# A decoder of twelve stages on one core: an opening with plain-f32 value tiles, codebook weights decoded a stage earlier, and a narrow cross-attention that works in pairs of tiles

## What is computed

```python
def _L2_xattn_ref(q, k, v, w_q, w_k, w_v, w_out, mask):      # 32 heads of 16, 8 key/value groups
    query, key, value = q @ w_q.T, k @ w_k.T, v @ w_v.T
    ...
    scores = jnp.einsum('bghnd,bgsd->bghns', query, key) / D_HEAD ** 0.5
    scores = jnp.where(mask, scores, jnp.finfo(scores.dtype).min)
    attention = jax.nn.softmax(scores, axis=-1)
    out = jnp.einsum('bghns,bgsd->bghnd', attention, value)
    return out.transpose(0, 3, 1, 2, 4).reshape(b, n, D_MODEL) @ w_out.T

def _L3_xattn_ref(hidden_states, cross_attention_states, attention_mask, ...):   # 32 heads of 128, 8 groups
    q, k, v = ...                                            # projections, then rmsnorm of q and k
    scores = jnp.einsum('bhqd,bhkd->bhqk', q, k) * scale + attention_mask
    attn = jax.nn.softmax(scores.astype(jnp.float32), axis=-1)
    out = jnp.einsum('bhqk,bhkd->bhqd', attn, v)
    return out... @ o_proj_w.T

def _L3_ffn_ref(x, codebooks, bias, ln_weight, codes, centroids):
    cw = _expand(centroids, codebooks)                       # 32 centroids, looked up in codebooks
    dots = x2 @ cw.T                                         # then normalised, softmax, > 0.5
    qmask, cmask = jnp.any(m, axis=-1), jnp.any(m, axis=0)
    W = _expand(codes, codebooks)                            # 512 x 512 weights, looked up too
    y = x2 @ W.T + bias
    return y * (qmask[:, None] & kmask[None, :])
```

## Time and profile before

| what | value |
|---|---|
| three runs | 1671.37, 1674.64, 1674.88 us; median 1674.64 |
| the profiled execution | 1671.8 us, its span 1670.0, mean granted clock 0.984 |
| PE busy | 1556.8 us (93%), 7321 matmuls |
| DVE busy | 1012.7 us (61%) |
| ACT busy | 889.4 us (53%) |
| POOL busy | 364.9 us (22%) |
| DMA | 165.38 MB, mean 99 GB/s |

### The profile page before, as it was taken

How to read it: one execution, slowest core, us unless ns; L and a number is a source line. 1 busy time by engine, 2 the same in 40 slices (tenths; PEclk the granted TensorE clock), 3 DMA queues, 4 the chain that set the end, 5 groups by cost and what they waited for, 6 DMA issues and landing times. The chain is left out here.

```text
span 1670.0 us, 22556 instructions
## 1 busy us (share of the span) xinstructions
PE 1556.8 (93%) x7321; PEld 1153.7 (69%) x7321; DVE 1012.7 (61%) x2105; ACT 889.4 (53%) x1625; POOL 364.9 (22%) x312
## 2 busy tenths in 40 slices
PE   7999999999998989898889996997999999999986
PEld 5878777877874444586566664875777787777864
DVE  3036777776676863374388873655067667766663
ACT  4235666555655441364158884552266667666661
POOL 0001111110112330153146663540011011111010
PEclk9999999999999999998999998999999999999999
DMA  9431222111165008262362202536311112211012
GB/s 311 128 114 57 83 75 82 57 57 57 50 252 194 26 26 296 87 213 72 93 153 30 33 16 87 171 123 239 113 64 57 45 68 82 75 57 57 26 59 80
DMA packets 82007, 165.38 MB, mean 99 GB/s; under 512 B 6752, under 2 KB 48864, under 8 KB 72464
## 3 DMA queue, kind: packets, MB, share of 16 engines
q1 hardware_dynamic: 81936, 164.50, 30.4%
HBM read 141.93 MB, written 17.04 MB: 95 GB/s over the span
## 5 line engine op out<-in xcount | busy, mean ns | idle before, releaser
L728 DVE TENSOR_TENSOR L0x_k_lo<-bank,L0x_k_hi 128x512 fp32r<-128x512 f32 x128 | 85.5, 687 | 55.4 <-ACT L0x_k_hi L630 55.4
L2558 POOL TENSOR_TENSOR L2x_p_lo<-L2x_e_t,L2x_p_hi 128x512 fp32r<-128x512 f32 x80 | 105.1, 1324 | 63.2 <-ACT L2x_p_hi L2743 62.2
L1358 DVE TENSOR_TENSOR L3x_k_lo<-bank,L3x_k_hi 128x512 fp32r<-128x512 f32 x128 | 86.1, 688 | 52.2 <-ACT L3x_k_hi L1247 51.8
L956 POOL TENSOR_TENSOR L3x_v_lo<-L3x_v_raw,L3x_v_hi 128x512 fp32r<-128x512 f32 x32 | 40.5, 1301 | 308.3 <-ACT L3x_v_hi L1238 308.3
L357 POOL TENSOR_TENSOR L0x_v_lo<-L0x_v_raw,L0x_v_hi 128x512 fp32r<-128x512 f32 x32 | 40.5, 1298 | 297.5 <-ACT L0x_v_hi L621 297.5
L630 ACT ACTIVATE L0x_k_hi<-bank 128x512 fp32r<-128x512 f32 x128 | 74.3, 598 | 52.9 <-PE bank L503 52.3
L2786 DVE CUSTOM_DVE_ANT_0 L2x_junk<-bank,L2x_mask 128x512 f32<-128x512 f32 x128 | 85.2, 688 | 19.8 <-PE bank L2644 10.1
L1247 ACT ACTIVATE L3x_k_hi<-bank 128x512 fp32r<-128x512 f32 x128 | 74.1, 604 | 41.5 <-PE bank L1116 41.2
L1347 DVE CUSTOM_DVE_ANT_0 L3x_s<-bank,L3x_mask 128x512 f32<-128x512 f32 x128 | 80.8, 687 | 3.9 <-PE bank L1020 1.7
L717 DVE CUSTOM_DVE_ANT_0 L0x_s<-bank,L0x_mask 128x512 f32<-128x512 f32 x128 | 80.8, 687 | 3.9 <-PE bank L430 2.0
L624 ACT ACTIVATE L0x_s<-L0x_s,L0x_neg_max 128x2048 f32<-128x2048 f32 x32 | 64.3, 2009 | 30.1 <-DVE L0x_neg_max L721 30.1
(11 more groups left out here) (649 smaller groups left out, 4426.5 us busy)
## 6 DMA issues: line engine op xcount, KB each, us to landing
L0x_w_q<-in_L0x_kq SPq DMA_DIRECT2D x8, 1024.0 KB, 5.4
L0x_values<-L0x_v_raw SPq DMA_DIRECT2D x32, 256.0 KB, 2.2
L0x_w_o<-in_L0x_o SPq DMA_DIRECT2D x8, 1024.0 KB, 4.8
L0x_v_raw<-L0x_values SPq DMA_DIRECT2D x8, 1024.0 KB, 4.8
L1a_w_o<-in_L1a_o SPq DMA_DIRECT2D x8, 1024.0 KB, 7.1
L2a_w_o<-in_L2a_o SPq DMA_DIRECT2D x8, 1024.0 KB, 7.3
L3x_w_q<-in_L3x_kq SPq DMA_DIRECT2D x8, 1024.0 KB, 5.4
L3x_w_o<-in_L3x_o SPq DMA_DIRECT2D x8, 1024.0 KB, 4.8
```

What stands on the lines that cost most here:

```text
L728: dve.tensor_tensor(p_lo[:, kt % 4, :], ring_bank(kt)[:], bits(p_hi[:, kt % 4, :]), ALU.subtract).then_inc(p_ready, 1)
L1358: dve.tensor_tensor(p_lo[:, kt % 4, :], ring_bank(kt)[:], bits(p_hi[:, kt % 4, :]), ALU.subtract).then_inc(p_ready, 1)
L2558: pool.tensor_tensor(p_lo[:, t % 8, :], e_of(t), bits(p_hi[:, t % 8, :]), ALU.subtract).then_inc(low_pool, 1)
```

## The change

In L3x `PLAIN = 3` value tiles are plain f32 matmuls, the first of them ahead of the turning of x, and `keep_clock` goes. Four slices of `v_raw` hold the kept tiles; hence the first load of values goes behind the stores. The queries are projected after tile 3 and their squares summed after tile 8.

The codebook has a class of its own. Its loads are issued with those of L3a; POOL makes the marks at the end of L3x; the decode's four steps are placed in L3a (three) and at the start of L3f (one), in banks 6 and 7, where the first and last take the place of `keep_clock`.

In L2x two tiles make a step u: exponential, rounding and low half are of 128x1024. The exponential goes always to one of three buffers in SBUF; POOL has pairs 0, 2, 3, 4 and 6 of a group (none of the last group), DVE 1, 5 and 7. `take_max` is of 128x1024, from banks 4 and 5 as a single pair (in the first group in turn with 2 and 3). Scores are issued twelve pairs ahead, the spread goes to the output's bank in step 6 of a group, the values are weighed three steps later, and the values' copy goes from DVE to ACT.

```diff
+    PLAIN = 3
...
-        v_tile = (o_t, rinv)
+        v_tile = [v_raw[:, 4 * b:4 * b + 4, :] for b in range(4)]
...
+                core.codebook.mark(pool)
...
-                load_v(0)
-                load_k_weights(1)
-                load_q_weights(1)
                 for i in range(KT):
+                    if i == 8:
+                        load_k_weights(1)
+                        load_q_weights(1)
                     sp.wait_ge(tile_kept, i + 1)
                     sp.dma_start(values.place(KT + i),
-                                 v_tile[i % 2][:].rearrange("p (g d) -> p g d", g=HG)).then_inc(tile_stored[i % 2], 16)
-                for b in range(2):
-                    sp.wait_ge(tile_stored[b], KT // 2 * 16)
+                                 v_tile[i % 4]).then_inc(tile_stored[i % 4], 16)
+                for b in range(4):
+                    sp.wait_ge(tile_stored[b], KT // 4 * 16)
+                load_v(0)
...
-                norm.keep_clock(pe)
-                norm.tensor(pe)
...
-                    if kt % 4 == 0:
...
+                        if kt < PLAIN:
+                            mm = pe.matmul(ring_bank(kt)[:], s_sb[:, c, keys], w_v[:, c, :], start=(c == 0),
+                                           stop=(c == CT - 1))
...
-                    if first:
-                        pe.wait_ge(tile_kept, KT)
-                    else:
+                    if not first:
                         pe.wait_ge(p_ready, g * 16)
                     for n in range(NC):
+                        if first:
+                            pe.wait_ge(tile_kept, KT - 3 + n)
...
-                pe.wait_ge(wv_kept, 1)
+                pe.wait_ge(w_v_in, 16)
+                pe.wait_ge(ctx_in[0], 16)
                 for kt in range(KT):
+                    if kt == PLAIN:
+                        pe.wait_ge(wv_kept, 1)
+                    if kt >= PLAIN and (kt == PLAIN or kt % 4 == 0):
+                        pe.wait_ge(ctx_kept, kt // 4 + 1)
                     project_values(kt)
-                    if kt == 2:
+                    if kt == 0:
+                        norm.tensor(pe)
+                    if kt == 3:
                         project_q(0)
-                    if kt == 5:
+                    if kt == 8:
                         sum_q_squares(0, used=False)
                 group(0, first=True)
...
+                split_context(0)
+                split_context(1)
+                keep_tile(0)
+                keep_tile(1)
+                split_context(2)
+                keep_tile(2)
+                split_context(3)
                 split_w(0)
...
+    def issue(self, sp):
+        sp.dma_start(self.codes[:], self.a["L3f_codes"]).then_inc(self.loaded, 16)
+        sp.dma_start(self.entry[:], self.a["L3f_entry"]).then_inc(self.loaded, 16)
+        sp.dma_start(self.books[:], self.a["L3f_books"]).then_inc(self.loaded, 16)
...
+    def mark(self, pool):
+        pool.wait_ge(self.loaded, 48)
+        for j in range(self.BG):
+            pool.tensor_scalar(self.hot[:, j, :], self.codes[:, j, :], self.entry[:], None,
+                               ALU.is_equal).then_inc(self.hot_ready, 1)
+
+    def tensor(self, pe, t):
+        pe.wait_ge(self.hot_ready, 2 * t + 2)
+        if t > 0:
+            pe.wait_ge(self.w_copied, t)
+        big, small = self.core.bank[6], self.core.bank[7]
+        for j in range(2):
+            pe.matmul(big[:], self.books[:, 2 * t + j, :], self.hot[:, 2 * t + j, 0:D], start=(j == 0), stop=(j == 1))
+        for j in range(2):
+            mm = pe.matmul(small[:, 0:self.N], self.books[:, 2 * t + j, :], self.hot[:, 2 * t + j, D:],
+                           start=(j == 0), stop=(j == 1))
+        mm.then_inc(self.w_ready, 1)
+
+    def scalar(self, act, t):
+        act.wait_ge(self.w_ready, t + 1)
+        act.activation(self.w_t[:, t, 0:D], self.core.bank[6][:], ACT.Copy)
+        act.activation(self.w_t[:, t, D:], self.core.bank[7][:, 0:self.N], ACT.Copy).then_inc(self.w_copied, 1)
...
-                norm.keep_clock(pe)
+                codebook.tensor(pe, 0)
                 norm.tensor(pe)
...
+                codebook.tensor(pe, 1)
                 pe.wait_ge(qk_biased, 2)
                 pe.matmul(core.bank[2][:, 0:P], qk_t[:, 0, :], qk_t[:, 1, :], start=True,
                           stop=True).then_inc(s_ready, 1)
+                codebook.tensor(pe, 2)
...
+                codebook.scalar(act, 0)
+                codebook.scalar(act, 1)
...
-                norm.keep_clock(pe)
+                codebook.tensor(pe, 3)
...
-        s_bank = lambda n: core.bank[4 + n % 2]
...
+        s_pair = lambda m: 2 if m % 2 and m < PAIRS else 4
...
+        by_pool = lambda u: u < (NG - 1) * PAIRS and u % PAIRS in POOL_PAIRS
+        pool_count = lambda u: sum(by_pool(i) for i in range(u))
+        dve_count = lambda u: u - pool_count(u)
...
+        scored = lambda u: PAIRS + 2 if u < 0 else min(NG * PAIRS, u + AHEAD + 1, PAIRS + 3 + 2 * u)
...
+                    if m >= PAIRS:
+                        pe.wait_ge(s_read, m)
+                    elif m >= 2:
+                        pe.wait_ge(s_read, m - 1)
...
+                def turned_scores(u):
+                    g, i = u // PAIRS, u % PAIRS
+                    if u >= 2:
+                        pe.wait_ge(exp_done, u - 1)
...
+                for u in range(NG * PAIRS + LAG):
+                    if u < NG * PAIRS:
+                        turned_scores(u)
+                    if u % PAIRS == PAIRS - 2 and u // PAIRS + 1 < NG:
+                        spread_max(u // PAIRS + 1)
+                    if u >= LAG:
+                        weigh(u - LAG)
+                    for m in range(scored(u - 1), scored(u)):
+                        score(m)
...
+                def exponential(u):
+                    act.wait_ge(st_ready, u + 1)
+                    if u >= 3:
+                        wait_low(act, u - 3)
+                    act.activation(e_t[u % 3][:].rearrange("p k n -> p (k n)"), pair(2 * (u % 2)),
+                                   ACT.Exp).then_inc(exp_done, 1)
+
+                def round_p(u):
+                    act.wait_ge(exp_done, u + 1)
+                    if u >= 4:
+                        act.wait_ge(pv_done, u - 3)
+                    act.activation(p_hi[:, p_at(u), :], e_t[u % 3][:], ACT.Copy).then_inc(hi_ready, 1)
...
+                    at = slice(i % 2 * 1024, i % 2 * 1024 + 1024)
+                    dve.tensor_tensor_reduce(junk[:], pair(s_pair(m)), bits(mask_sb[:, at]), 1.0, LOWEST, ALU.add,
+                                             ALU.max, part_max[:, i // 2, i % 2:i % 2 + 1]).then_inc(s_read, 1)
...
+                for u in range(NG * PAIRS + 1):
+                    g, i = u // PAIRS, u % PAIRS
+                    for m in range(scored(u - 2), scored(u - 1)):
+                        take_max(m)
+                        if m % PAIRS == PAIRS - 1:
+                            take_row_max(m // PAIRS)
+                    low_half(u - 1)
+                    if i == PAIRS - 1 and g + 1 < NG:
+                        keep_max(g + 1)
```

326 lines of the change are left out of this document (142 added, 184 removed).

## The result

The changed kernel takes 1655.26 us (median of four runs, 1653.65 to 1656.75) against 1674.76 before (four runs, 1671.37 to 1676.2). The quotient of these medians is 0.9884; the ratio on record is 0.9903, interval 0.9885 to 0.9922. It is faster, but by 16 to 20 us where 28.6 were forecast. One execution further down, of the kernel with both edits (1803.50 us at a granted clock of 0.84), is left out of its median as a slow one.

What follows compares the result with a forecast made beforehand. PE was taken as busy nearly throughout, with gaps to win in L3x's opening, L3f and L2x. -11.8 - 9.4 - 6 = -27.2 from 1671.8 gives 1644.6; forecast 1646 us, range 1637 to 1657.

Steps and rivals of the forecast that it cites:

- Part A: L3x's opening: first value matmul to K projection takes 52.2 us instead of 64.0, so -11.8; nothing lost behind it.
- Part B: Codebook marks on POOL and decodes moved: L3a +3.0 us, L3f -12.4, together -9.4.
- rival 2: Half clock in L3x's opening (-1.5 for -11.8) or L3f (-3.3 for -9.4): 1652 to 1656 us, chance 0.15.
- The bounds for a mark: End of L3x on POOL: one codebook comparison of 128x544 takes 1.04 to 1.43 us.
- the point from which it would count (4.0): POOL's codebook marks: from 4.0 us per mark the last decode would be late.
- Part C: L2x in pairs of tiles: 20.5 us per group instead of 21.2, and a shorter end, in sum -6 us.
- rival 1: L2x gains nothing, as DVE and POOL hold one another or the single score bank pair costs: 1652 to 1657, chance 0.22.
- The first steps bring nothing: L2x's start: two scores per step through one pair of banks eat what the shorter prologue saves.
- held up to 1.5 us ... I take 0.8: L2x groups: POOL's doubled instruction holds DVE's diagonal; spread and next maximum late by 0.5 to 1.2 us, 0.8 taken.
- The floor of 19.7: L2x: PE's own matmuls and spread need 19.7 us per group, the least a group can take.
- the upper bound for DVE (19.3): L2x: DVE's work per group takes 16.3 to 19.3 us, just under PE's.
- The 1.9 us "beside POOL": L2x: one DVE low half was taken as 1.23 us alone and 1.9 beside POOL.

Runs made afterwards that it cites:

- the kernel with both edits: The whole change with L2x's diagonal in four one-input DVE instructions and a second pair of score banks in the first group: 1.0040 of before, median 1678.57 us.
- fillers: Extra identity matmuls in L3x's last group, then also at L2x's end, on the whole change with diagonal on ACT and second score banks: 0.9830, then 0.9834 of before.
- the four instructions: The whole change with L2x's diagonal made by four 128x128 DVE instructions with one tensor input each, instead of one with two: 1.007 of before, median 1681.65 us.
- the runs of the parts: The kernel before with one part alone: Part A 0.9947 (1664.24 us), Part B 0.9940 (1662.26), Part C 1.0014 (1674.74), against 1672.30.

## Why the prediction was right or wrong

*Part A.* Each duration of the sum held, and the sum: 52.3 us for 52.2. Two things outside the sum didn't. The 64.0 that it was set against contained 2.5 us of half clock that isn't always there: -9.1 to -11.6, not -11.8. And what lies behind the opening was put at nothing: all nine kernels with part A and no fillers lose 1.3 to 2.5 us at L3x's end, in after in matmuls at half clock; the three without part A don't. In after the first group loses another 1.7 at half clock, so L3x is 8.5 shorter in all. That cost wasn't on the list: the rival had half clock in the opening only. Why the clock falls behind these gaps with part A and not without it stays open.

*Part B.* +2.9 and -12.2 were measured where +3.0 and -12.4 were forecast, with the clock at 1.00. In after the clock fell in L3f's first microseconds, which was rival 2, for 1.7 us. The bounds for a mark were too low (1.65, not 1.04 to 1.43), at no cost, as the point from which it would count (4.0) was far.

*Part C* is where the forecast went wrong: +1.3 instead of -6 in the two profiles, rival 1. The terms, after against before:
- prologue and first group: the first spread comes 39.9 us after the stage's start for 41.8, -1.9, and the first group takes 24.2 for 19.5, +4.7. The failing step is "The first steps bring nothing", which lets the two cancel and has no size for either; together they cost 2.8. Each of the two double steps took 2.3 us more than a single one, through one pair of banks, and the second another 0.4 at half clock.
- groups 1 to 6: 124.8 for 127.3, -2.5; forecast -5.4. The failing step is "held up to 1.5 us ... I take 0.8". The diagonal was held 1.74, and the group is 1.4 longer than with the diagonal on ACT, 1.15 of it as one idle gap of PE. The floor of 19.7, the place of the hold and the diagonal as its victim were right; the size was not. Taking a middle of 0.5 to 1.2 for PE's loss wasn't backed by a row: of holds of 0.7 and 1.7 us, 0.4 and 1.4 went to PE. The first five of these six gain nothing; the 2.4 that were won are in the last, 18.8 long, at whose end no scores are left to make (1.2 were forecast there).
- last group and end: 37.9 for 36.9, +0.9; forecast -0.5. ACT works through the last group without a pause, and its last rounding ends 22.7 us after the last spread, 21.3 before; DVE's low half of 1024 comes behind it (1.23 us), so the last weighing ends 1.8 later. The output matmuls, with less half clock, give 0.9 back.

One row was misread. The 1.9 us "beside POOL" is an instruction that takes so long with POOL idle, as its first in before shows:

```profile
570.02 1.89 DVE L1731 TENSOR_TENSOR L0a_prod<-L0a_qkv,L0a_s 128x1024 f32<-128x1024 f32 x1
...
572.05 2.86 POOL L1636 TENSOR_TENSOR L0a_prod_pool<-L0a_qkv,L0a_s 128x1024 f32<-128x1024 f32 x1 [13.76 <-DVE L0a_prod L1731]
```

It was no sign of a hold, and the upper bound for DVE (19.3) rests on it; the sum doesn't.

The rule of the Trainium skill that the prediction set against this part ("SBUF — State Buffer", SBUF: two separate sides) agrees: the one that comes second waits for the whole instruction of the first, as the diagonal's end, 0.56 us after POOL's, shows. It speaks of two SBUF inputs or a two-port mode of DVE, and has `tensor_scalar`, the form of the four instructions, among those that can enter such a mode. That the four were held is what their run showed; whether by such a mode no run here shows. DVE's low halves were not held, as forecast: POOL is idle when they are due.

*Sum.* In the two profiles A gave -8.5 for -11.8, B -7.7 for -9.4 and C +1.3 for -6; 5.8 less in stages ahead of L2x and 2.6 more in L2a and L2f come from no edit. By the runs of the parts, A is -8.1, B -10.0 and C +2.4 us by medians: -15.7, and the whole change is -16 to -20. Rival 1 had 1652 to 1657, and the time is 1655.26; its cause is the one given there for half of it (the hold), and the single pair of banks for the other, in the first group alone. That the time lies in its range is in part luck, as it had A and B in full. The lower end of the range, 1637, doesn't follow from its terms, which give 1646 - 4.5 = 1641.5; nothing hangs on it.

## What to carry to other kernels

Before work is given to POOL in longer instructions, look for each DVE instruction that must be on time, has its inputs in SBUF, and is of a form that was held here (two inputs, or one input times a column), and ask which POOL instruction will be running when it starts: its wait is the rest of that instruction, and most of it is passed on to whoever waits for DVE. To split such an instruction can make it worse, as each piece may meet an instruction of POOL. Here it was best moved to ACT, even though ACT is slower at it (1.26 us against 0.69) and the busier engine in these groups (18.1 us against 16.4). And when work is fetched ahead through one buffer, the catching-up phase runs at the buffer's round trip (2.32 us here), not at the busy time of either engine: give that phase its own buffers.

## What the runs showed of the hardware

- Idle gaps of the same length ahead of the same matmuls are followed by half clock in one kernel and not in another (L3x's end: 1.77 us of idle, then 0.61 after, 1.00 before). Stages with unchanged code differ by 1 to 4 us with it: L1a took 99.1 us in after, with no stretch at half clock, and 103.1 in before, with 10.2 us of them. So a single profile's stage lengths can't tell effects of that size.
- An instruction of DVE with two SBUF inputs (128x512, 0.69 us alone) that started under one of POOL ended 0.55 us after POOL's did: 1.41 us beside instructions of 128x512, 2.4 beside those of 128x1024.
- A one-input f32 instruction of DVE, 128x128 and 0.28 us alone, took up to 2.42 beside POOL, and four in a row were done only when POOL's run of three was over. A reduction of 128x8 to 128x4, also all in SBUF, took its 0.16 beside POOL as alone.
- POOL compares 128x544 codes with a column in 1.65 us, where DVE took 3.38 us for all eight on the time line of before.
